# Partial contexts of a block added in double-width pairs, on GpSimd and, for the last block, on VectorE

## What is computed

```
x = x + gnn(layernorm(x))         # 4 heads of 32, keys in 8 chunks of 128
x = x + ffn(layernorm(x))         # each token goes to 2 of 8 experts, hidden width 256

scores = clip(q k / sqrt(32), -10, 10), -10 where the adjacency is 0     # (n, j, c)
attn   = softmax over c alone                                            # one sum for each chunk j
ctx    = sum over j and c of attn * v                                    # 8 chunks are added
gnn    = layernorm(ctx Wo + bo + x) * gamma + beta
```

## Time and profile before

| | |
|---|---|
| median of 3 runs | 776.33 us (773.45 to 777.26) |
| the profiled execution | 776.3 us |
| its span | 774.2 us |
| TensorE busy | 698.8 us (90%) |
| VectorE busy | 623.0 us (80%) |
| GpSimd busy | 580.1 us (75%) |
| ScalarE busy | 495.4 us (64%) |

### The profile page before, as it was taken

The page is one execution under the profiler, slowest core; times in us unless marked ns, Lnnn a source line. Parts: engine busy times, 40 slices in busy tenths (PEclk is TensorE's granted clock), DMA queues, the critical chain, the costliest instruction groups (busy, mean ns, idle before and its releaser), DMA issues.

```text
span 774.2 us, 17066 instructions
## 1 busy us (share of the span) xinstructions
PE 698.8 (90%) x5416; PEld 363.3 (47%) x5416; DVE 623.0 (80%) x1455; ACT 495.4 (64%) x898; POOL 580.1 (75%) x689
## 2 busy tenths in 40 slices
PE   4897999999999999999999999886968869999994
PEld 2222233333333333333333333231668769999994
DVE  4699999999999999999999999899784535545552
ACT  3665567777677776777767776553766426666662
POOL 7569495989879898798987988958477445667664
PEclk9999999999999999999999999997999979999998
DMA  7530000011010110101100001040323223333330
GB/s 264 191 93 28 1 29 14 21 35 47 23 44 21 35 47 23 43 21 36 44 26 29 21 23 42 15 138 29 94 61 92 77 80 88 94 86 99 97 92 1
DMA packets 47959, 45.42 MB, mean 59 GB/s; under 512 B 6982, under 2 KB 42577, under 8 KB 47873
## 3 DMA queue, kind: packets, MB, share of 16 engines
q1 hardware_dynamic: 41888, 31.60, 14.5%
q0 software_dynamic: 5984, 12.74, 4.5%
HBM read 27.73 MB, written 18.34 MB: 60 GB/s over the span
## 4 chain that ended last, share of the span: by engine, by line
PE 43%; DVE 28%; issue 17%; POOL 6%; DMA 2%; ACT 2%; DVEq 1%; POOLq 0%; ACTq 0%
DVE e L940 12%; PE scores_ps L436 11%; PE ctx_ps L448 8%; PE z_ps L455 7%; PE scores_ps L600 5%; POOL out L1412 5%; DVE ctx_part L948 4%; PE ctx_ps L626 3%; PE z_ps L626 3%; DMA near<-in_x 2%; DVE ln_stats L906 2%; PE job_ps L490 2%; PE job_ps L485 2%; DVE best_at L996 1%; DVE z_part L953 1%
## 5 line engine op out<-in xcount | busy, mean ns | idle before, releaser
L739 ACT ACTIVATE e<-e 128x2048 f32<-128x2048 f32 x128 | 244.4, 1910 | 141.5 <-DVE e L940 134.3
L940 DVE SCALAR_TENSOR_TENSOR e<-scores_ps,bound_mem 128x2048 f32<-128x2048 f32 x128 | 292.2, 2283 | 24.6 <-PE scores_ps L436 22.9
L824 ACT ACTIVATE e<-scores_ps,bound_mem 128x128 f32<-128x128 f32 x364 | 104.0, 372 | 67.5 <-PE scores_ps L600 65.0
L1412 POOL DMA_INDIRECT out<-e,near x91 | 91.0, 1000 | 69.1 <-POOL near L1405 27.0
L455 PE MATMUL z_ps<-e,one_column 128*32 128x512 f32 x1024 | 135.5, 601 | 0.0
L1385 POOL TENSOR_TENSOR ctx_part<-ctx_part,z_inv 128x1024 f32<-128x1024 f32 x60 | 114.9, 1914 | 24.7 <-DVE z_inv L956 23.8
L1397 POOL TENSOR_TENSOR ctx_sum<-ctx_sum,ctx_part 128x512 f32<-128x512 f32 x90 | 115.7, 1286 | 6.0
L600 PE MATMUL scores_ps<-e,bound_mem 128*128 128x128 f32 x728 | 100.2, 282 | 2.5 <-DVE bound_mem L1117 1.0
L600 PEld LDWEIGHTS scores_ps<-e,bound_mem 128*128 128x128 f32 x728 | 91.5, 197 | 5.0 <-issue 4.1
L948 DVE STREAM_TRANSPOSE ctx_part<-ctx_ps 128x512 f32<-128x512 f32 x128 | 90.3, 706 | 1.4 <-PE ctx_ps L448 1.3
L1359 POOL DMA_INDIRECT sorted_rows<-x_rows,slot x64 | 63.4, 991 | 18.6 <-issue 17.3
(11 more groups left out here) (171 smaller groups left out, 1031.0 us busy)
## 6 DMA issues: line engine op xcount, KB each, us to landing
near<-sorted_rows SPq DMA_DIRECT2D x91, 130.0 KB
near<-in_x SPq DMA_DIRECT2D x16, 256.0 KB, 2.8
bound_mem<-in_adjT SPq DMA_DIRECT2D x4, 1024.0 KB, 10.5
x_post<-in_x SPq DMA_DIRECT2D x16, 256.0 KB, 2.8
sorted_rows<-pad_row SPq DMA_DIRECT2D x1, 3640.0 KB, 14.9
out<-e,near POOLq DMA_INDIRECT x91
sorted_rows<-x_rows,slot POOLq DMA_INDIRECT x64
bound_mem<-in_w SPq DMA_DIRECT2D x1, 1024.0 KB, 6.6
```

The source lines that it names most:

```text
L739: nc.scalar.activation(every, every, ACT.Exp, scale=SCORE_SCALE).then_inc(exp_done, 1)
L824: nc.scalar.activation(e_flat[:, h_at:h_at + P], scores_ps[:, i % 2, k * P:(k + 1) * P], ACT.Gelu, bias=part_flat[:, bias_at:bias_at + 1]) ...
L940: dve.scalar_tensor_tensor(out=e[:, s % E_RING], in0=scores_ps[:], scalar=-CLIP, in1=to, op0=ALU.max, op1=ALU.min).then_inc(clipped, 1)
L1412: nc.gpsimd.indirect_dma_start(out=out_rows, out_offset=bass.IndirectOffsetOnAxis(ap=near_u[:, id_at:id_at + 1], axis=0), in_=e_flat[:, at ...
```

## The change

Eight additions' worth of work is regrouped. `add_pair(v, j)`, for j = 2, 4, 6, adds the pair of slots j - 2, j - 1 onto the pair j, j + 1, in place in `ctx_part`, 1024 elements. `add_halves(v)` then adds the two halves of the last pair into `ctx_sum`, 512 elements. So a block has four additions in place of seven, and `ctx_added` counts four a block. The order on GpSimd becomes scale 0, scale 2, pair 2, scale 4, pair 4, scale 6, pair 6, halves, with the other work where it was: in most blocks layer norm 2 now stands after pair 2, `add_residual` after scale 4, `root_both` after scale 6. `turn` waits for the pair addition that consumes its slot, so slots 0 and 1 come free after pair 2, and the last two after the halves. For block 15 VectorE does the same.

```
         def ctx_pair(v, j):
             at = (CHUNKS * v + j) % PARTS
             return ctx_part[:, at:at + 2]

 turn:
-                    need(dve, ctx_added, (CHUNKS - 1) * u + max(j, 1))
+                    need(dve, ctx_added, CHUNKS // 2 * u + j // 2 + 1)

 VectorE, block 15 (slots k of the expert phase):
+            def add_last_pair(j):
+                v = BLOCKS - 1
+                to, frm = ctx_pair(v, j), ctx_pair(v, j - 2)
+                dve.wait_ge(last_scaled, j // 2 + 1)
+                need(dve, ctx_added, CHUNKS // 2 * v + j // 2 - 1 if j > 2 else 0)
+                dve.tensor_tensor(to, to, frm, ALU.add).then_inc(ctx_added, 1)
+            def add_last_halves():
+                v = BLOCKS - 1
+                pair = ctx_pair(v, CHUNKS - 2)
+                need(dve, ctxT_ready, v - 1)
+                dve.wait_ge(ctx_added, CHUNKS // 2 * (v + 1) - 1)
+                dve.tensor_tensor(ctx_sum[:, v % 2], pair[:, 0], pair[:, 1], ALU.add).then_inc(ctx_added, 1)
 before add_bias(k - 2):
                 if k == 4:  scale_last(2)
-                    add_last(1)
                 if k == 5:  scale_last(4)
-                    add_last(3)
                 if k == 6:  scale_last(6)
-                    add_last(5)
 after add_bias(k - 2):
-                k == 4: add_last(2)     k == 5: add_last(4)     k == 6: add_last(6), add_last(7)
+                k == 4: add_last_pair(2)  k == 5: add_last_pair(4)  k == 6: add_last_pair(6), add_last_halves()
 turn_sum:
-                dve.wait_ge(ctx_added, (CHUNKS - 1) * (v + 1))
+                dve.wait_ge(ctx_added, CHUNKS // 2 * (v + 1))

 GpSimd:
+            def add_pair(v, j):
+                to, frm = ctx_pair(v, j), ctx_pair(v, j - 2)
                 pool.wait_ge(ctx_scaled, CHUNKS // 2 * v + j // 2 + 1)
+                need(pool, ctx_added, CHUNKS // 2 * v + j // 2 - 1 if j > 2 else 0)
+                nc.gpsimd.tensor_tensor(to, to, frm, ALU.add).then_inc(ctx_added, 1)
+            def add_halves(v):
+                pair = ctx_pair(v, CHUNKS - 2)
+                need(pool, ctxT_ready, v - 1)
+                pool.wait_ge(ctx_added, CHUNKS // 2 * (v + 1) - 1)
+                nc.gpsimd.tensor_tensor(ctx_sum[:, v % 2], pair[:, 0], pair[:, 1], ALU.add).then_inc(ctx_added, 1)
                 if is_block(u - 1):
-                    add_context(u - 1, 1)
                     scale(u - 1, 2)
...
-                    add_context(u - 1, 2)
+                    add_pair(u - 1, 2)
...
-                    add_context(u - 1, 3)
                     scale(u - 1, 4)
...
-                    add_context(u - 1, 4)
-                    add_context(u - 1, 5)
+                    add_pair(u - 1, 4)
                     scale(u - 1, 6)
...
-                    add_context(u - 1, 6)
-                    add_context(u - 1, 7)
+                    add_pair(u - 1, 6)
+                    add_halves(u - 1)
```

More of the change, by code:

```diff
@@ L228, in graph_transformer_layer, with ctx_pair @@
         job_ps = [bank(f"job_ps{k}", [P, BLOCK]) for k in range(2)]
+        def ctx_pair(v, j):
+            at = (CHUNKS * v + j) % PARTS
+            return ctx_part[:, at:at + 2]
         def turned_x2_ps(v):
@@ L959, in scale_last @@
             def scale_last(j):
-                at = (CHUNKS * (BLOCKS - 1) + j) % PARTS
-                pair = ctx_part[:, at:at + 2]
+                pair = ctx_pair(BLOCKS - 1, j)
                 dve.wait_ge(z_inverted, BLOCKS)
@@ L965, in scale_last @@
                                   ALU.mult).then_inc(last_scaled, 1)
-            def add_last(j):
+            def add_last_pair(j):
                 v = BLOCKS - 1
-                to, at = ctx_sum[:, v % 2], (CHUNKS * v + j) % PARTS
+                to, frm = ctx_pair(v, j), ctx_pair(v, j - 2)
                 dve.wait_ge(last_scaled, j // 2 + 1)
[L971 to L977, removed]
+                need(dve, ctx_added, CHUNKS // 2 * v + j // 2 - 1 if j > 2 else 0)
[6 more added lines that the diff above has]
+                dve.tensor_tensor(ctx_sum[:, v % 2], pair[:, 0], pair[:, 1], ALU.add).then_inc(ctx_added, 1)
             def turn_sum(v):
-                dve.wait_ge(ctx_added, (CHUNKS - 1) * (v + 1))
+                dve.wait_ge(ctx_added, CHUNKS // 2 * (v + 1))
                 need(dve, proj_filled, v)
@@ L1232, in _ @@
                 if k == 4:
-                    add_last(2)
+                    add_last_pair(2)
                 if k == 5:
-                    add_last(4)
+                    add_last_pair(4)
                 if k == 6:
-                    add_last(6)
-                    add_last(7)
+                    add_last_pair(6)
+                    add_last_halves()
                 if k == 10:
@@ L1382, in scale @@
                     pool.wait_ge(ctx_turned, CHUNKS * (v + 1))
-                at = (CHUNKS * v + j) % PARTS
-                pair = ctx_part[:, at:at + 2]
+                pair = ctx_pair(v, j)
                 nc.gpsimd.tensor_tensor(pair, pair, z_inv[:, v % 2, j:j + 2].to_broadcast([P, 2, SQUARES, DH]),
                                         ALU.mult).then_inc(ctx_scaled, 1)
-            def add_context(v, j):
-                to, at = ctx_sum[:, v % 2], (CHUNKS * v + j) % PARTS
+            def add_pair(v, j):
+                to, frm = ctx_pair(v, j), ctx_pair(v, j - 2)
                 pool.wait_ge(ctx_scaled, CHUNKS // 2 * v + j // 2 + 1)
[L1391 to L1397, removed]
+                need(pool, ctx_added, CHUNKS // 2 * v + j // 2 - 1 if j > 2 else 0)
[5 more added lines that the diff above has]
+                nc.gpsimd.tensor_tensor(ctx_sum[:, v % 2], pair[:, 0], pair[:, 1], ALU.add).then_inc(ctx_added, 1)
             def mask_id(i):
```

## The result

The changed kernel took 788.81 us (median of 6 runs, 786.16 to 791.71), the kernel before beside it 776.74 us (6 runs, 773.45 to 779.43): a ratio of 1.0164, 95% interval 1.0135 to 1.0192. It is 12 us slower, and the forecast, 776.2 us within 772.5 to 780.0, was wrong. The profiled executions have spans of 774.2 and 789.0 us, 14.8 apart.

What follows compares the result with a forecast made beforehand. It took TensorE and VectorE, handing the chain to each other, as the bound, with GpSimd mattering through holds of VectorE. Block 1 +1.2, block 15 -1.0 and VectorE's sum -0.3 gave -0.1 us: 776.2 us, range 772.5 to 780.0.

Steps and rivals of the forecast that it cites:

- A wide addition, 2.37 us (1.91 to 2.57): On GpSimd: 1024 elements take 0.20 us fixed plus twice a narrow addition's rest, between a scaling and two narrow additions.
- Steady blocks, priced at nothing: Steady blocks: the sum is ready 0.63 us later, 0.49 us of spare stay, so VectorE's own work hides it.
- If that cover is gone: Steady blocks: without spare, `turn_sum` is late and delays the next clip and scores, 1:1 in some 12 blocks.
- the late sum: Steady-block rival, chance 0.05: wide additions from 2.86 us make each sum late; at 3.1 us it costs 2.9 us.
- Block 1, +1.2 (0 to +2.8): Block 1: reordered GpSimd scalings and additions hold VectorE's sum_biases, with TensorE waiting behind; taken as +1.2 us.
- the prediction's first case: Block 1: scaling 2 goes ahead of VectorE's 640 elements, then turns follow; +1.5 us, against +0.8 if VectorE wins.
- Block 15, -1.0 (-2.0 to +1.5): Block 15: layer norm 2 starts 0.95 us earlier and x_rows, ending VectorE's last hold, comes earlier; taken as -1.0 us.
- the rule that the two engines take turns whole instruction by whole instruction: GpSimd and VectorE operations on SBUF alternate by whole instructions; in block 15 t_col may be held 2.2 us.
- the later holds end with x_rows all the same: Block 15: a 2.2 us hold of t_col mostly moves waiting forward, as VectorE's later holds still end with x_rows.
- VectorE's own sum, -0.3: Block 15's sum on VectorE, which TensorE awaits 4.22 us: pairs shorten it by 0.3 us (-1.4 to +0.8).
- Holds cost more than they give: Rival, chance 0.15: block 1's scaling 2 wins, block 15's clip is held 1.5 us without return; +2.7 to +4 us.

Runs made afterwards that it cites:

- e7: Changed kernel plus two short GpSimd waits in block 15, for its own wide addition before the third and fourth scaling: 780.09 us, ratio 1.0068 to the kernel before.
- e2: Kernel before with only block 0 added in pairs, the other blocks as before: 779.61 us, ratio 1.0023 to the kernel before.
- e5: Changed kernel plus a tiny 1.05 us GpSimd pow ahead of each block's first scatter up to block 13: 784.16 us, ratio 1.0122 to the kernel before.
- e6: Changed kernel with the addition of beta ahead of the scatters, not behind, up to block 13: 784.86 us, ratio 1.0124 to the kernel before.

## Why the prediction was wrong

*A wide addition, 2.37 us (1.91 to 2.57).* Right: most rows show 2.37 or 2.38, the mean is 2.398. 0.2 us fixed and twice the rest of a narrow one was a good rule.

*Steady blocks, priced at nothing.* The steps that the prediction wrote down came as described: GpSimd waits for ln_var ahead of root_both (idle 1.25 us), the sum is ready ahead of `turn_sum` (0.26 us spare, 0.49 forecast), the wait of `turn` costs nothing. The step that failed is the one that wasn't made. The argument followed the sum to its reader and stopped, but the sum isn't the last thing in GpSimd's block: four scatters and add_beta stand behind it, and they moved too, by 0.88 us against VectorE. "If that cover is gone" was answered for `turn_sum` only. Nothing in the trace before tells that a scatter later by 0.9 us can cost, since there its release, an estimate of 2.95 + 1.85 = 4.8 us from the rows after, lies within the reciprocal, and VectorE comes to the clip at 5.20 all the same. What could have been seen is that a moved instruction with a DMA behind it was given no line in the sum, and the range had no term for nine steady blocks but the late sum, with a chance of 0.05.

*Block 1, +1.2 (0 to +2.8).* +1.92 (2.08 with the start of the program), within its bounds: scaling 2 won its race, for the reason given (it waits for nothing). The 640 elements took 2.54 us and the 512 elements 1.88, and the two later ones were held less than before, 1.02 and 0.55 us; the four differences sum to +1.85. That is the prediction's first case played out, turn by turn, which it put at +1.5 (its four terms add up to +1.4). Taking the middle of two cases cost 0.7 us.

*Block 15, -1.0 (-2.0 to +1.5).* It was +4.95. The prediction asked the right question, whether t_col is held, and answered "2.2 us" from the rule that the two engines take turns whole instruction by whole instruction. It took 6.00, since the turn didn't change at three ends of instructions that were followed without a gap, and the next hold came on top, not in its place: "the later holds end with x_rows all the same" failed, because VectorE, 6 us late, now ran beside the next row of GpSimd's instructions, and `owner` ended with the fourth scaling, at 543.53 + 1.92 = 545.45. The Trainium skill, page "SBUF — State Buffer", section "Who interferes with whom", has the holder keep the pair for the whole instruction and lets issue order decide; by that alone t_col would have ended behind the first wide addition at 534.2, as it does in e7. The traces agree where GpSimd leaves a gap and at some places where it doesn't (`begin_col` in e2), but not here.

A second half of that step has no row and wasn't priced: with VectorE held, TensorE was busy for 0.82 of 4.5 us, and in the next window its granted clock was 0.50.

*VectorE's own sum, -0.3.* -0.41, the pairs 1.21 and 1.22 us, the two holds 1.08 and 0.89 us; TensorE's wait for ctxT is 3.81 in place of 4.22.

*The rivals.* "Holds cost more than they give" named the place and the sign of two of the three losses, +7 us, with a price of +2.7 to +4 and a chance of 0.15. In block 1 the rule of the turns gave the size; in block 15 the size fell with that rule: in its own terms the highest point was a sum of single instructions. "The sum is late" named the third place for a reason that didn't happen.

## What to carry to other kernels

When an operation on an engine is moved or resized, follow everything queued behind it to the next idle time of that engine, its DMAs too, and not only to the reader of its result. A row of GpSimd instructions without a gap can be one long hold for a VectorE operation that reads two SBUF tensors; a wait on one's own last result, 0.08 us, cuts it, and it is worth placing where VectorE's short operations are on the path. Where phases of 0.3 us decide between 0 and 6 us, a block that wins alone (0.9975) can lose among others, so the change is to be measured whole.

## What the runs showed of the hardware

- GpSimd can keep a VectorE operation on SBUF waiting over several of its instructions if they follow without a gap: a 0.15 us subtraction of VectorE took 6.00 us (6.00 and 6.01 in e5 and e6), and 2.80 with a gap of 0.08 us put into the row. It doesn't always: `begin_col` in e2 was let through at 527.85 between two instructions that overlap by 0.04 us.
- A VectorE operation can be caught from within an indirect DMA's instruction on GpSimd: t_col asked 0.56 us into one of 0.96 us and stayed held until 537.4, at 0.25 us into one it passed. In both, the next GpSimd instruction followed at once. Being within the DMA's instruction is not enough: in e7 two operations asked 0.69 and 0.88 us into one (539.73 and 539.92) and took their free 0.15 us; there GpSimd's next instruction came 0.3 us after its end. Whether the DMA or what follows it does the catching isn't shown.
- The completion of TensorE's matmuls reached VectorE up to 1.4 us behind their modelled end (1.1 in the row shown, 0.14 elsewhere) in 37 blocks where the fourth of four indirect DMAs had started shortly before that end, 1.77 to 2.00 us behind the DMA's start; the matmuls themselves went on (388.89, 0.07 us before the modelled end of the scores). Five blocks with such a start were spared. The Trainium skill, page "SBUF — State Buffer", section "Who interferes with whom", says that TensorE and ScalarE never wait on anyone; that holds for the engine's work here, and not for when another engine learns of it.
- A GpSimd addition of 1024 elements a partition with two full inputs takes 2.37 us, against 1.91 with a broadcast second input.
